# Writing the Gelu-plus-residual sum in block order and letting the second centring read it in token order, in a one-core S5 block

## The reference, cut to what matters

```
g  = group norm of x (32 groups of 3 channels)
fx = layernorm over the 96 channels of g, with gain ln1_g and bias ln1_b
xs = linear scan over the 256 tokens of each batch, 48 complex modes, input B_bar fx
y  = gelu(2 Re(C xs) + D fx) + fx
fy = layernorm over channels of y, with gain ln2_g and bias ln2_b
z1, z2 = split(fy W_enc^T);  z = z1 * gelu(z2)
out = x + z W_dec^T + fy
```

## Time and profile before

| | |
|---|---|
| median of three runs (lowest, highest) | 120.13 us (119.25, 121.56) |
| span of the profiled execution | 118.2 us, 1793 instructions |
| TensorE matmul busy | 103.6 us (88%), 648 instructions |
| TensorE weight load busy | 66.4 us (56%) |
| VectorE busy | 79.4 us (67%), 279 instructions |
| ScalarE busy | 42.4 us (36%) |
| GpSimd busy | 30.2 us (26%) |
| chain that ended last | TensorE 66%, VectorE 18%, issue 6%, DMA 5% |
| mean granted TensorE clock | 0.971 |

### The profile page before, as it was taken

The page is one execution under the profiler, slowest core; times in us unless marked ns, Lnnn a source line. Parts: engine busy times, 40 slices in busy tenths (PEclk is TensorE's granted clock), DMA queues, the critical chain, the costliest instruction groups (busy, mean ns, idle before and its releaser), DMA issues.

```text
span 118.2 us, 1793 instructions
## 1 busy us (share of the span) xinstructions
PE 103.6 (88%) x648; PEld 66.4 (56%) x648; DVE 79.4 (67%) x279; ACT 42.4 (36%) x79; POOL 30.2 (26%) x25
## 2 busy tenths in 40 slices
PE   0349999999999998798987999957999999999980
PEld 0349977898778752665523469635333863453310
DVE  0769993675989398766997248899620256797480
ACT  2184155721819200150243690350069303113310
POOL 8400000400009970000316000165930000079000
PEclk9999999999999999999999999997559999999999
DMA  3995000000000000000000000000000000062036
GB/s 102 271 242 107 3 0 0 6 0 0 0 0 6 0 0 3 0 0 0 6 0 0 3 0 0 6 0 0 0 0 0 0 0 0 24 177 70 0 85 181
DMA packets 3736, 3.81 MB, mean 32 GB/s; under 512 B 464, under 2 KB 3632, under 8 KB 3728
## 3 DMA queue, kind: packets, MB, share of 16 engines
q1 hardware_dynamic: 3392, 3.50, 11.4%
q10 hardware_dynamic: 336, 0.21, 0.7%
HBM read 2.13 MB, written 1.57 MB: 31 GB/s over the span
## 4 chain that ended last, share of the span: by engine, by line
PE 66%; DVE 18%; issue 6%; DMA 5%; ACT 1%; SPq 1%; DVEq 1%
PE ps L416 66%; DVE w L638 6%; DMA xs<-x_dram 5%; DVE y L961 2%; DVE rs L668 2%; DVE parts L880 1%; DVE rs L638 1%; DVE st L810 1%; DVE fy L638 1%; DVE sq L638 1%; SPq L239 1%; DVE parts L642 1%; ACT y L377 1%; ACT gl L371 1%; DVEq L90 1%
## 5 line engine op out<-in xcount | busy, mean ns | idle before, releaser
L416 PE MATMUL ps<-sq,mt 96*32 96x64 f32 x256 | 17.7, 236 | 0.0
L416 PEld LDWEIGHTS ps<-sq,mt 96*32 96x32 f32 x256 | 16.7, 122 | 1.7 <-issue 1.5
L416 PE MATMUL ps<-fy,mt 96*96 96x512 f32 x32 | 16.7, 658 | 0.7 <-DVE fy L638 0.7
L293 POOL TENSOR_TENSOR res<-fy,xs 96x512 f32<-96x512 f32 x8 | 10.7, 1358 | 19.1 <-DVE fy L638 19.1
L638 DVE SCALAR_TENSOR_TENSOR w<-ps,vecs,y 96x512 f32<-96x512 f32 x8 | 6.0, 746 | 11.4 <-ACT y L377 11.4
L377 ACT ACTIVATE y<-ps,vecs 96x512 f32<-96x512 f32 x8 | 5.5, 684 | 22.6 <-PE ps L416 22.6
L285 POOL TENSOR_TENSOR y<-gl,fx 96x512 f32<-96x512 f32 x4 | 5.9, 1474 | 29.7 <-ACT gl L371 29.7
L416 PE MATMUL ps<-xs,pm 96*96 96x256 f32 x32 | 11.5, 516 | 0.0
L416 PE MATMUL ps<-mt 96*96 96x96 f32 x38 | 7.0, 375 | 4.8 <-DMA mt<-mats_dram 4.8
L371 ACT ACTIVATE gl<-ps,db 96x512 f32<-96x512 f32 x8 | 5.5, 682 | 13.3 <-PE ps L416 13.3
L416 PEld LDWEIGHTS ps<-fy,mt 96*96 96x96 f32 x32 | 5.4, 176 | 8.4 <-issue 7.3
(11 more groups left out here) (108 smaller groups left out, 156.3 us busy)
## 6 DMA issues: line engine op xcount, KB each, us to landing
out_dram<-sq SPq DMA_DIRECT2D x8, 192.0 KB, 2.3
xs<-x_dram SPq DMA_DIRECT2D x3, 384.0 KB, 6.8
xs<-x_dram SPq DMA_DIRECT2D x2, 192.0 KB, 3.3
mt<-mats_dram SPq DMA_DIRECT2D x1, 347.6 KB, 7.6
mt<-mats_dram ACTq DMA_DIRECT2D x1, 180.0 KB, 3.6
sm<-small_dram ACTq DMA_DIRECT2D x1, 8.6 KB, 2.6
cmask<-mask_dram ACTq DMA_DIRECT2D x1, 12.0 KB, 4.6
```

Of the source, the lines that this page charges most:

```text
L293: nc.gpsimd.tensor_tensor(cols(res, H, i), cols(fy, H, i), xs[:, HB * H + 2 * i:HB * H + 2 * i + 2, :].rearrange("c n l -> c (n l)"), ALU. ...
L416: return nc.tensor.matmul(o, lhsT, rhs, start=start, stop=stop)
```

## The change

`y2` stays in block order: both `second_input` functions now write contiguously, tile i to tile i. `center(H, i)` reads the 512 tokens of tile i out of the block-ordered buffer: 64 values of m, and for each the 8 values of b, which lie 256 elements (1 KiB) apart. Its output in PSUM is as before, contiguous and in token order. Waits, semaphores and the order of the work are unchanged, and so is the number of instructions.

```
@@ GpSimd, second_input(H)
-                yv = y2[:, H, :].rearrange("c (m b) -> c b m", b=T)
                 for i in (0, 2):
                     pool.wait_ge(gl_ready, NT * H + i + 1)
-                    nc.gpsimd.tensor_tensor(
-                        yv[:, RT * i:RT * (i + 1), :], cols(gl, H, i).rearrange("c (b m) -> c b m", b=RT),
-                        cols(fx, H, i).rearrange("c (b m) -> c b m", b=RT), ALU.add).then_inc(y2_pool, 1)
+                    nc.gpsimd.tensor_tensor(cols(y2, H, i), cols(gl, H, i), cols(fx, H, i),
+                                            ALU.add).then_inc(y2_pool, 1)
@@ TensorE, center(H, i)
-                mm(bank(H, i)[0:96, :], m(M_P), cols(y2, H, i)).then_inc(centered[1], 1)
+                tokens = y2[:, H, :].rearrange("c (b m) -> c m b", b=T)[:, TILE // T * i:TILE // T * (i + 1), :]
+                mm(bank(H, i)[0:96, :].rearrange("c (m b) -> c m b", b=T), m(M_P), tokens).then_inc(centered[1], 1)
@@ VectorE, second_input(H, i)
                 dve.wait_ge(gl_ready, NT * H + i + 1)
-                yv = y2[:, H, :].rearrange("c (m b) -> c b m", b=T)
-                nc.vector.tensor_tensor(
-                    yv[:, RT * i:RT * (i + 1), :], cols(gl, H, i).rearrange("c (b m) -> c b m", b=RT),
-                    cols(fx, H, i).rearrange("c (b m) -> c b m", b=RT), ALU.add).then_inc(y2_vec, 1)
+                nc.vector.tensor_tensor(cols(y2, H, i), cols(gl, H, i), cols(fx, H, i), ALU.add).then_inc(y2_vec, 1)
```

## The result

The changed kernel took 127.80 us (median of four runs, 127.67 to 129.26) against 120.04 us for the kernel before. The ratio is 1.077, 95% interval 1.065 to 1.090. The forecast was 119.0 us with a range up to 124.8. The profiled execution of the changed kernel took 127.78 us, with a span of 125.9 us, so 1.9 us lie around the span. Its span is 7.7 us longer than the one before. All ratios and intervals in this document leave out executions that took over 1.5 per cent longer than the fastest of the same kernel, while medians and listed times are of all executions.

A forecast was written before the change was run, and what follows sets the result against it. The chain was taken to run through VectorE's sums into TensorE, which alone holds the last 30.25 us. Gains of 0.75 (half 0) and 0.34 (half 1), nothing for TensorE's stepped reads: 120.13 - 1.1 = 119.0 us, range 117.0 to 124.8.

The forecast's parts named there:

- VectorE's sums, 0.39 us less each: VectorE's four sums: with a contiguous write each falls from 1.075 us to 0.69 us.
- the 1.1 us of the sum: Total forecast gain on the span: 0.75 us from half 0 plus 0.34 us from half 1.
- GpSimd's sums at no gain: GpSimd's four sums: a contiguous write saves 12 ns each, counted as zero.
- Half 0 starts 0.75 earlier: TensorE's centring of half 0 starts 0.77 us earlier, counted as 0.75 because its own `seed_sum` is late next.
- Half 1 0.34 us earlier: In half 1, VectorE's shorter sum of tile 1 moves `encode(0, 0)` from 81.82 to 81.48, 0.34 us.
- This slack is why I take zero: TensorE's sixteen centrings: operand needed at most every other clock at 2.4 GHz, so the 1 KiB step costs nothing.
- the far bound: Upper bound for TensorE's stepped read: VectorE's 1.82 ns per element as column floor, adding 0.98 ns at full clock.
- Rival 1: TensorE pays for the stepped centring reads: 5.6 us more less 1.1 gained, 4.5 us slower, 124.6 us; chance 0.24.
- Rival 2: Shorter idle gaps lessen TensorE's clock dip around 81 to 88 us: 115.9 us if prevented, 117.4 if halved; chance 0.13.
- half of 3.1: Rival 2's halved dip: the half-level clock costs TensorE 3.1 us in that stretch; halving it gives 117.4 us.

The follow-up runs named there:

- writes alone: Changed kernel, but the centring reads its 512 columns contiguously as in the kernel before; ratio 0.988 to the kernel before, median 118.79 us.
- reads alone: Kernel before, sums still written with the 32-byte step, but the centring reads with a step of 1 KiB; ratio 1.082 to the kernel before.
- four steps: Four kernels differing only in the centring's operand: columns 8, 12, 16 bytes apart, or pairs 1 KiB apart; spans 116.5, 117.8, 127.4, 116.2 us.
- twice: Sums written in block order, each of the eight centring matmuls issued twice, reading contiguously; four executions: 122.95, 125.86, 126.30, 126.62 us.
- in a row: Changed kernel, but in half 0 the four centrings come first and half 1's four doublings after, not in turns; ratio 1.119, median 135.1 us.
- the mixed order: Changed kernel, but `encode(0, 1)` stands between the second and third centring of half 1; four executions: 124.64, 128.93, 129.20, 129.44 us.

## Why the prediction was wrong

- **VectorE's sums, 0.39 us less each: right.** 1.075 to 0.680 us. The writes alone measured 1.4 us (0.2 to 2.5) against the 1.1 us of the sum.
- **GpSimd's sums at no gain: right**, 1.277 to 1.262 us.
- **Half 0 starts 0.75 earlier: right, with a little luck in the number.** The start moved by 0.77 us, but 0.10 of that was there already at `seed_sum`; counted from there, the gain is 0.67. TensorE's own `seed_sum` was indeed late next: VectorE's sum ended at 64.09, before it, and left the chain.
- **Half 1 0.34 us earlier: right**, 0.31.
- **"This slack is why I take zero": wrong, and it is the step that failed.** The argument was that a float32 column every other clock of 2.4 GHz leaves time for a jump, and so the term for TensorE's sixteen instructions was put at nothing. It measured 5.55 us. The runs showed 1.69 ns for each 16-byte stretch touched, two full column times. Contiguous float32 puts four columns in such a stretch and needs a new one each 3.4 ns; two columns per stretch are just free; one is twice too slow. VectorE's stepped write, 1.82 ns per element, was the nearest row and was taken for the far bound. GpSimd was no evidence against it: at 2.5 ns per element it would hide a price of that size.
- **Rival 1 (124.6 us, 0.24) was the mechanism that happened, and its size for the matmuls was right**: 5.6 us, measured 5.55. It still missed by 3 us. Missing was the term for what stands behind: the granted clock fell during the stepped centring of half 1, which cost 3.67 us on `encode(0, 1)` and the variances.
- **Rival 2 looked at the clock from the wrong side.** It asked whether a shorter idle gap would save the dip. The first stretch was indeed half as long in the profiled execution, but it won 0.49 us on `encode(0, 0)` and not half of 3.1, since the stepped centring takes 0.865 us at either level; and with the writes alone, where the gap is as short, it was not halved. The new cost did not come after idle time: it came after matmuls that are busy in the trace, each at half the contiguous pace. The prediction treated the clock as a matter of gaps alone.

The stretches add up to the whole 7.7 us. Shown: the read is the cause (writes alone, reads alone), the price goes by 16-byte stretches (four steps), the clock's second fall goes with the stepped runs and not with their length or place (twice, in a row). Open: by what means the slow reads bring the clock down, what brings it back, why the first stretch is sometimes half as long, and why one execution in four of the mixed order escapes.

## What to carry to other kernels

When a permutation can sit on any of several accesses, price it at each: here it cost VectorE's write 0.39 us per 512 columns, GpSimd's write nothing, TensorE's read 0.86 us per float32 matmul of 512 columns plus the clock, and TensorE's write to PSUM nothing. Keep at least two neighbouring float32 columns together in a moving operand, if it reads across a step; with pairs it was free here at a distance of 1 KiB. And an engine that cannot show a price because it is slower than it is no evidence that the price is absent. Last, a step behind the changed one can pay too: here 3.67 of the 9.22 us that the reads cost fell on matmuls that the change does not touch.

## What the runs showed of the hardware that was not expected

- A float32 matmul's moving operand costs 1.69 to 1.76 ns for each different 16-byte stretch, where the contiguous pace does not hide it: 0.45, 0.67, 0.90 and 0.865 us per instruction of 512 columns at steps of 8, 12, 16 bytes and 1 KiB, at the full level of the clock, against 0.43 contiguous. At 1 KiB the half level gives the same 0.865 us.
- A step of 32 bytes on the PSUM write of a float32 matmul is free: 592 ns as for the contiguous one.
- The granted clock can fall while TensorE is busy without a gap: 3.4 us of stepped centring at 2.4 GHz, then ten microseconds at 1.2 GHz in the changed kernel, and almost 14 us in half 0 when eight such instructions stood in a row.
